# A fused decoder layer on one core: the stacked rows of keys and queries written from SBUF part by part, instead of through a scratch in DRAM

## Chip, core and metric

One core of one Trainium2 chip. The metric is the device time of one launch, in microseconds (us). The profiler's execution is one launch; its span runs from the first to the last instruction.

## What is computed

One decoder layer over 16 items (batches) of 256 tokens and 256 channels: a gated recurrence with quantised weights, cross attention to a context with 16 heads of 16 channels, and a three-layer network; after each a layer norm. The change is in the attention:

```
Q = (query @ Wq.T + bq).reshape(b, sq, H, D).transpose(0, 2, 1, 3)
K = (key @ Wk.T + bk).reshape(b, sk, H, D).transpose(0, 2, 1, 3)
V = (value @ Wv.T + bv).reshape(b, sk, H, D).transpose(0, 2, 1, 3)
Q = apply_rope(Q, cos_q, sin_q)
K = apply_rope(K, cos_k, sin_k)
scores = jnp.einsum('bhqd,bhkd->bhqk', Q, K) * SCALE
scores = jnp.where(mask[:, None, None, :] == 0, neg_inf, scores)
attn = jax.nn.softmax(scores, axis=-1)
out = jnp.einsum('bhqk,bhkd->bhqd', attn, V)
```

## The kernel before

One item g (0 to 15) is one round of a software pipeline; several items are in work at once, and one leaves about every 49.5 us. Every engine runs a fixed list of steps. The list comes from the table `TIMES` (a start time for each step on each engine, relative to `BEGIN[g]`); `order(engine)` sorts the steps of all items by it. The times in the table only set the order; the waits are semaphores. TensorE takes its matmuls strictly in that order.

Keys and queries are float32 after the rotary step and are cut into three bf16 parts whose sum is the value. ScalarE rounds part 0 (step `kp` or `qp`, function `first_part`, L768). VectorE takes the rest and rounds part 1 (`k_parts`, `q_parts`: L1384, L1386, L1400, L1401). Part 2 is the last remainder, for K on GpSimd (`kparts_`, L604), for Q on VectorE (L1402). The tiles `kpart` and `qpart` are [128, 3, 2, 256]: channel c*128+p in partition p of chunk c. A channel index is d*16+h, for d the channel in its head and h the head.

A score is a matmul over stacked rows. `k_st` and `q_st` (two buffers each, for even and odd items) hold in partition 16*s+d, for slot s of six, the part `PARTS_K[s]` or `PARTS_Q[s]` of channel d of all 16 heads: 8 KB for one partition. Row 96 of `k_st` is the mask row. Rows 97 and 98 of `q_st` get the high and low part of the row maximum (`maxrow`, L462, DMAs from `m_hi` and `m_lo`).

`PARTS_Q = (0, 0, 1, 0, 2, 1)` and `PARTS_K = (0, 1, 0, 2, 0, 1)`: part 0 fills three slots, part 1 two, part 2 one.

The stacks are filled by SyncE. `kput` and `qput` (L424, L425) wait for part 2 and write all three parts into a DRAM scratch `scr`, 768 rows of 512 B in one DMA. `kget` and `qget` wait for the landing of that DMA and then issue six DMAs, one for each slot (`stack`, L436): 16 partitions x 8 KB, each partition a contiguous 8 KB in DRAM. `kget` also issues the mask row (L446). The first score tile of an item (`score`, un = 0; its matmuls are L1021) waits for both stacks, `kst_in` and `qst_in`. Later the shifted scores (`shifted`, L1040) wait for `max_in`, the two rows of `maxrow`.

SyncE's order around one item: `loadc`, `maxrow(g-1)`, `kput(g)`, `kget(g)`, `store`, `loadx`, `qput(g)`, `qget(g)`, `loadc`, `maxrow(g)`. A tile of parts is not written again before the scratch DMA that reads it has landed (`kout`, `qout`).

Of the kernel before, what the change touches and what calls it, by code (L numbers as in the profile page):

```python
# [8 lines left out]
BF16 = mybir.dt.bfloat16  # L9
# [3 lines left out]
ALU = mybir.AluOpType  # L13
# [4 lines left out]
P = 128  # L18
NB, S, D = 16, 256, 256
H, DH = 16, 16  # L20
# [4 lines left out]
T = S  # L25
G = NB
NT = T // P
CT = D // P
# [7 lines left out]
PARTS_Q = (0, 0, 1, 0, 2, 1)  # L36
PARTS_K = (0, 1, 0, 2, 0, 1)
# [31 lines left out]
    max2 V62.116 | stat2 G77.947 | round2 V62.352 | rqT P70.375 A74.82 | gate0 P73.784 A75.992 V74.417  # L69
    gate1 P75.073 A76.687 V79.484 | stat3 G95.369 | round3 V80.455 | sqT P81.141 A83.767 | down P83.188 V84.911  # L70
    bn V89.51 G98.004 | x1 V94.309 | kT P64.537 A74.926 | v P55.644 A57.034 | rotk G88.907
    kp A81.655 V82.304 G95.379 | kput S81.174 | kget S97.725 | x1T P84.601 A88.953 | xb G103.696 | q P89.268 A92.187
    rotq G127.27 V96.241 | qp A93.161 V97.684 | qput S116.099 | qget S116.444 | score0 P115.878 V110.409
    score1 P116.97 V115.546 | score2 P119.918 V115.793 | score3 P120.171 V117.492 | score4 P125.547 V117.94
    score5 P126.961 V121.024 | score6 P129.726 V124.461 | score7 P130.83 V124.53 | max P131.852 A132.889 V126.824
    maxrow S133.847 | exp0.0 P133.871 A136.815 | exp0.1 P134.243 A139.205 | pv0 P136.736 | exp1.0 P135.426 A139.693
    exp1.1 P136.729 A139.73 | pv1 P137.231 A141.48 | exp2.0 P137.075 A140.898 | exp2.1 P137.429 A141.482
    pv2 P143.82 | exp3.0 P140.189 A142.702 | exp3.1 P142.471 A144.878 | pv3 P144.83 A145.892
    oTok P146.421 V149.661 | oT P150.162 A147.86 | wo P153.238 V157.354 | bn2 V159.204 G182.428 | x2 V160.758
# [108 lines left out]
def build(nc, A, out):  # L188
    with ExitStack() as ctx:
        def sb(name, shape, dt):  # L190
            return ctx.enter_context(nc.sbuf_tensor(name, shape, dt))

        def sem(name):
            return ctx.enter_context(nc.semaphore(name))

        def count(name, per=1):
            return Count(sem(name), per)
# [64 lines left out]
        kt1 = sb("kt1", [P, 2, T], F32)  # L262
        kt2 = sb("kt2", [P, 2, T], F32)
        krest = sb("krest", [P, CT, T], F32)
        kpart = sb("kpart", [P, 3, CT, T], BF16)
        v_aug = pair("v_aug", [P, NT, H, VW], F32)
        x1T = sb("x1T", [P, CT, T], F32)
        qb = sb("qb", [P, 2, T], F32)
        qt1 = sb("qt1", [P, 2, T], F32)
        qt2 = sb("qt2", [P, 2, T], F32)  # L270
        qrest = sb("qrest", [P, CT, T], F32)
        qpart = sb("qpart", [P, 3, CT, T], BF16)
        q_all = sb("q_st", [P, 2, H, T], BF16)
        k_all = sb("k_st", [P, 2, H, T], BF16)
        q_st = [q_all[:, i] for i in range(2)]
        k_st = [k_all[:, i] for i in range(2)]
# [39 lines left out]
        mneg = oS[0:NB, 1, 0:S // 2].bitcast(BF16)  # L316
        bvT = oS[:, 2:4, 0:P]

        scr = nc.dram_tensor("scr", [2, 2, 3, D, T], BF16).ap()
        mscr = nc.dram_tensor("mscr", [NB * S], BF16).ap()  # L320

# [26 lines left out]
        mx3, sc3, q3 = count("mx3"), count("sc3"), count("q3")  # L349
        mv_s, rstd_s, x1_s, xb_s = (count(n) for n in ("mv_s", "rstd_s", "x1_s", "xb_s"))  # L350
        kt_s, kh_s, kr_s, kp1_s, kparts = (count(n) for n in ("kt_s", "kh_s", "kr_s", "kp1_s", "kparts"))
        qs_s, qr_s, qh_s, qparts = (count(n) for n in ("qs_s", "qr_s", "qh_s", "qparts"))
        kout, qout = count("kout", 16), count("qout", 16)
        kst_in, qst_in = count("kst_in", (len(PARTS_K) + 1) * 16), count("qst_in", len(PARTS_Q) * 16)
        mhi_s, max_in, pv_s = count("mhi_s"), count("max_in", 2 * 16), count("pv_s", 2)
        mv2_s, rstd2_s, x2_s, xh_s = (count(n) for n in ("mv2_s", "rstd2_s", "x2_s", "xh_s"))
        h0h_s, h1h_s = count("h0h_s", KT // 2), count("h1h_s", KT // 2)
# [18 lines left out]
        def _(sp):  # L376
# [40 lines left out]
                sp.wait_ge(mask_s_, 1)  # L417
                sp.dma_start(mscr.rearrange("(b s) -> b s", s=S), mneg).then_inc(mask_out, 16)

            def put(g, n, parts, made, gone):  # L420

                if g >= 2:
                    sp.wait_ge(*(kst_in, qst_in)[n].at(g - 2))
                sp.wait_ge(*made.at(g))  # L424
                sp.dma_start(scr[g % 2, n].rearrange("i (c p) t -> p (i c) t", p=P),  # L425
                             parts[:, :, :, :].rearrange("p i c t -> p (i c) t")).then_inc(gone.sem, 16)

            def kput(g):
                put(g, 0, kpart, kparts, kout)

            def qput(g):
                put(g, 1, qpart, qparts, qout)

            def stack(g, dst, n, which, arrived):
                for s, i in enumerate(which):
                    sp.dma_start(dst[DH * s:DH * (s + 1), :, :],  # L436
                                 scr[g % 2, n, i].rearrange("(d h) t -> d h t", d=DH)).then_inc(arrived.sem, 16)

            def kget(g):
                if g >= 2:  # L440
                    sp.wait_ge(*ringB.filled(g - 2, "exp3.1"))
                if g == 0:
                    sp.wait_ge(mask_out, 16)
                    sp.wait_ge(st_k, 1)
                sp.wait_ge(*kout.at(g))
                sp.dma_start(k_st[g % 2][R_MASK:R_MASK + 1, :, :],  # L446
                             mscr[g * T:(g + 1) * T].rearrange("(o t) -> o t", o=1)
                             .unsqueeze(1).broadcast_to([1, H, T])).then_inc(kst_in.sem, 16)
                stack(g, k_st[g % 2], 0, PARTS_K, kst_in)

            def qget(g):
                if g >= 2:
                    sp.wait_ge(*ringB.filled(g - 2, "exp3.1"))
                if g == 0:
                    sp.wait_ge(st_q, 1)
                sp.wait_ge(*qout.at(g))
                stack(g, q_st[g % 2], 1, PARTS_Q, qst_in)

            def maxrow(g):
                sp.wait_ge(*ringB.emptied(g, "max"))  # L460
# [8 lines left out]
            def later(load):  # L469
                return lambda g: load(g + 2) if g + 2 < G else None  # L470

            steps = {"w:mask": mask_row, "loadx": later(loadx), "loadc": later(loadc), "kput": kput, "kget": kget,
                     "qput": qput, "qget": qget, "maxrow": maxrow, "store": store}
            for step, g in order("SP"):
                steps[step](g)
            sp.wait_ge(*out_s.at(G - 1))
# [2 lines left out]
        def _(pool):  # L479
            own = Own(pool, own_p)  # L480
# [118 lines left out]

            def kparts_(g):  # L600
                if g >= 1:
                    pool.wait_ge(*kout.at(g - 1))
                pool.wait_ge(*kp1_s.at(g))
                pool.tensor_tensor(kpart[:, 2], krest[:, :, :], kpart[:, 1], ALU.subtract).then_inc(kparts.sem, 1)  # L604

# [12 lines left out]
            def norm3(g):  # L618
# [3 lines left out]
                for n in range(NT):  # L622
# [4 lines left out]
            steps = {"w:rope": spread, "w:down": down_weights, "w:wk": lambda g: in_order(w_k, kt1, wkv_in, 2, wk_s), "w:wq": lambda g: in_order(w_q, qt1, wq_in, 1, wq_s),  # L627
                     "scale": scale, "stat1": stat1, "stat2": stat2,
                     "stat3": stat3, "bn": norm1, "xb": xb, "rotk": rotk, "kp": kparts_, "rotq": rotq,
                     "bn2": norm2, "bn3": norm3}  # L630
# [4 lines left out]
        def _(act):  # L635
            own = Own(act, own_a)
# [127 lines left out]
            def first_part(g, turned, t, part, gone, done):  # L764
                if g >= 1:
                    act.wait_ge(*gone.at(g - 1))
                act.wait_ge(*turned.at(g))
                act.activation(part[:, 0], t[:, :, :], ACT.Copy).then_inc(done.sem, 1)  # L768
# [53 lines left out]
            def finish(g):  # L822
                i = g % 2
                act.wait_ge(*rstd3_s.at(g))
                for n in range(NT):
# [4 lines left out]
            steps = {"w:m": lambda g: magnitudes((0, 1), abs_act), "w:g1": sums, "w:g2": lambda g: magnitudes((3, 4), abs_act),  # L830
                     "w:bv": value_bias, "scale": squares1, "xqT": lambda g: unround(g, "xqT", xqT),
                     "iv0": lambda g: input_gate(g, 0), "iv1": lambda g: input_gate(g, 1), "a": decay_raw, "aT": decay,
                     "sq": complement, "rec": squares2, "rqT": lambda g: unround(g, "rqT", rqT),
                     "gate0": lambda g: gate(g, 0), "gate1": lambda g: gate(g, 1),
                     "sqT": sqT_,
                     "w:rope": angles, "w:bqk": qk_bias, "kT": keys, "v": values, "q": queries,
                     "kp": lambda g: first_part(g, kt_s, kt1, kpart, kout, kh_s), "x1T": x1T_,
                     "qp": lambda g: first_part(g, qr_s, qt1, qpart, qout, qh_s), "max": max_high,
                     "pv1": lambda g: weighted(g, 0), "pv3": lambda g: weighted(g, 2), "oT": oT_, "x2T": x2_high,
                     "out": finish}  # L840
            for c in range(KT // 2):
# [337 lines left out]
        def _(dve):  # L1179
            own = Own(dve, own_d)  # L1180
# [199 lines left out]
            def k_parts(g):  # L1380
                if g >= 1:
                    dve.wait_ge(*kparts.at(g - 1))
                dve.wait_ge(*kh_s.at(g))
                dve.tensor_tensor(krest[:, :, :], kt1[:, :, :], kpart[:, 0], ALU.subtract).then_inc(kr_s.sem, 1)  # L1384
                dve.wait_ge(*kr_s.at(g))
                dve.tensor_scalar(kpart[:, 1], krest[:, :, :], 1.0, None, ALU.mult).then_inc(kp1_s.sem, 1)  # L1386
# [8 lines left out]

            def q_parts(g):
                if g >= 1:
                    dve.wait_ge(*qout.at(g - 1))
                dve.wait_ge(*qh_s.at(g))
                own.settle(dve.tensor_tensor(qrest[:, :, :], qt1[:, :, :], qpart[:, 0], ALU.subtract))  # L1400
                own.settle(dve.tensor_scalar(qpart[:, 1], qrest[:, :, :], 1.0, None, ALU.mult))  # L1401
                dve.tensor_tensor(qpart[:, 2], qrest[:, :, :], qpart[:, 1], ALU.subtract).then_inc(qparts.sem, 1)  # L1402

            def score_largest(g, un):
# [120 lines left out]
```

## Time and profile before

| | us |
|---|---|
| median of 3 runs | 890.74 (890.59 to 890.93) |
| the profiled execution, its own time | 888.45 |
| its span | 886.7 |
| TensorE busy | 800.9 |
| VectorE busy | 642.4 |
| ScalarE busy | 549.2 |
| GpSimd busy | 296.9 |

The granted clock of TensorE is 0.998 of full speed over the span. DMA engines are busy for about 30% of it. A busy time is a sum over the whole span; what a wait costs is read in the order of time of one item. Item 8 (its first score at 471 us) stands for the middle of the run.

### The profile page before, as it was taken

Reading aid. Unit: us, or ns where it says so; the run is one execution under the profiler, and the core shown is the slowest. Engines: PE = TensorE matmul, PEld = TensorE weight load, DVE = VectorE, ACT = ScalarE, POOL = GpSimd, SP = SyncE. Lnnn points to the kernel's source line nnn. Section 1 sums busy time; section 2 is a strip of 40 time slices with the busy share of each in tenths; the row PEclk is TensorE's granted clock in tenths of the full one; section 3 lists DMA queues with packets and bytes.
Section 4 is the critical chain, followed back from the end, with each engine's and each line's share of the span. In section 5 each row is a group of like instructions: output and inputs, shape, how many; then the busy total and the mean of one; then the engine's idle time right before and its main releaser. Section 6 shows DMA issues by size and latency. Waiting matters only on the chain.

```text
span 886.7 us, 17907 instructions
## 1 busy us (share of the span) xinstructions
PE 800.9 (90%) x6856; PEld 626.3 (71%) x6890; DVE 642.4 (72%) x1224; ACT 549.2 (62%) x917; POOL 296.9 (33%) x476
## 2 busy tenths in 40 slices
PE   1687899999999999999999999999999999998986
PEld 1444477877877787877878777877777787876665
DVE  6658486886959596886959595977869595966442
ACT  4644857657494847667584848567584948573432
POOL 7753314152333324151433324151423334141001
PEclk9999999999999999999999999999999999999999
DMA  9033332415042332316042433415061423223000
GB/s 298 13 66 66 67 67 51 71 31 115 14 105 41 79 66 56 78 32 114 14 109 36 80 66 56 84 42 98 14 125 21 89 44 63 59 50 72 1 13 25
DMA packets 52517, 57.47 MB, mean 65 GB/s; under 512 B 7856, under 2 KB 48848, under 8 KB 49360
## 3 DMA queue, kind: packets, MB, share of 16 engines
q1 hardware_dynamic: 52432, 56.31, 30.0%
q8 instruction: 56, 0.92, 0.4%
q14 instruction: 29, 0.24, 0.1%
HBM read 39.24 MB, written 16.79 MB: 63 GB/s over the span
## 4 chain that ended last, share of the span: by engine, by line
PE 61%; DVE 16%; ACT 9%; DMA 4%; issue 4%; POOL 3%; SPq 1%; DVEq 0%; ACTq 0%; POOLq 0%
PE bankC L1118 18%; PE bankA L1053 6%; PE bankC L1102 6%; PE bankA L987 6%; PE slotB L1021 6%; PE slotB L1040 5%; PE bankA L922 5%; DMA q_st<-m_lo 4%; DVE u L1304 2%; ACT pr L794 2%; PE bankA L903 2%; DVE bn L1359 2%; ACT sqT L682 2%; ACT L794 2%; POOL rstd L574 2%
## 5 line engine op out<-in xcount | busy, mean ns | idle before, releaser
L1118 PE MATMUL bankC<-h0h,w 128*128 128x256 f16 x1024 | 233.7, 273 | 0.6 <-DVE h0l L1452 0.5
L1118 PE MATMUL bankC<-h0l,w 128*128 128x256 f16 x1024 | 233.3, 272 | 0.0
L1408 DVE TENSOR_REDUCE nmax<-slotB 128x4 f32<-128x1024 f32 x128 | 150.7, 1216 | 1.8 <-PE slotB L1021 0.3
L794 ACT ACTIVATE pr<-slotB 128x1024 f32<-128x1024 f32 x128 | 127.5, 1028 | 13.3 <-PE slotB L1040 13.0
L1118 PEld LDWEIGHTS bankC<-h0h,w 128*128 128x128 f16 x1024 | 99.9, 98 | 15.2 <-issue 1.2
L1118 PEld LDWEIGHTS bankC<-h0l,w 128*128 128x128 f16 x1024 | 100.1, 98 | 14.2
L1040 PE MATMUL slotB<-q_st,k_st 99*128 99x256 bf16 x512 | 74.7, 274 | 13.4 <-DMA q_st<-m_lo 11.2
L573 POOL TENSOR_SCALAR rstd<-mv 128x2 f32<-128x2 f32 x48 | 9.3, 193 | 215.6 <-DVE mv L1362 214.5
L1021 PE MATMUL slotB<-k_st,q_st 97*128 97x256 bf16 x512 | 76.7, 272 | 4.2 <-DVE nmax L1408 2.5
L1040 PEld LDWEIGHTS slotB<-q_st,k_st 99*128 99x128 bf16 x512 | 43.9, 97 | 38.3 <-DMA q_st<-m_lo 15.9
L1102 PE MATMUL bankC<-xh,w 128*128 128x256 f16 x256 | 57.8, 273 | 14.3 <-DVE xl L1446 13.7
L1392 DVE TENSOR_TENSOR qt<-qb,turn 128x512 f32<-128x512 f32 x16 | 11.1, 692 | 76.6 <-ACT qb L751 76.6
L819 ACT ACTIVATE h0h<-bankC 128x512 f16<-128x512 f32 x64 | 38.2, 597 | 44.8 <-PE bankC L1102 44.7
L1053 PE MATMUL bankA<-pr,v_aug 128*32 128x256 f32 x1024 | 65.4, 384 | 0.2 <-ACT pr L794 0.2
L1021 PEld LDWEIGHTS slotB<-k_st,q_st 97*128 97x128 bf16 x512 | 47.8, 97 | 17.9 <-DVE nmax L1408 3.9
L1134 PE MATMUL bankC<-w,h1h 128*128 128x256 f16 x256 | 59.0, 273 | 0.6 <-DVE h1l L1452 0.6
L1134 PE MATMUL bankC<-w,h1l 128*128 128x256 f16 x256 | 59.0, 273 | 0.0
L1102 PE MATMUL bankC<-xl,w 128*128 128x256 f16 x256 | 57.6, 272 | 0.0
L682 ACT ACTIVATE rqT<-bankA,cst 128x512 bf16<-128x512 f16 x16 | 11.0, 687 | 72.4 <-PE bankA L913 72.4
L819 ACT ACTIVATE h1h<-bankC 128x512 f16<-128x512 f32 x64 | 38.0, 594 | 28.9 <-PE bankC L1118 28.9
L1452 DVE SCALAR_TENSOR_TENSOR h1l<-bankC,h1h 128x512 f16<-128x512 f32 x64 | 42.7, 685 | 16.3 <-ACT h1h L819 16.3
L1452 DVE SCALAR_TENSOR_TENSOR h0l<-bankC,h0h 128x512 f16<-128x512 f32 x64 | 43.5, 685 | 6.5 <-ACT h0h L819 4.8
(206 smaller groups left out, 1752.0 us busy)
## 6 DMA issues: line engine op xcount, KB each, us to landing
k_st<-scr SPq DMA_DIRECT2D x96, 128.0 KB, 4.5
q_st<-scr SPq DMA_DIRECT2D x96, 128.0 KB, 4.3
scr<-kpart SPq DMA_DIRECT2D x16, 384.0 KB, 2.8
scr<-qpart SPq DMA_DIRECT2D x16, 384.0 KB, 2.7
x<-in_x SPq DMA_DIRECT2D x16, 256.0 KB, 3.7
cT<-in_ctxT SPq DMA_DIRECT2D x16, 256.0 KB, 2.7
out<-x SPq DMA_DIRECT2D x16, 256.0 KB, 2.2
pr<-in_k SPq DMA_DIRECT2D x1, 1024.0 KB, 9.6
```

The costliest lines, as they stand in the source:

```text
L794: act.activation(pr[i % 2][:, c, :, :].rearrange("p h s -> p (h s)"), slotB[ringB.slot(g, name)][:, :], ACT.Exp, scale=DH ** -0.5).then_in ...
L819: act.activation(flat(dst[:, 2 * m:2 * m + 2, :]), bankC[ringC.slot(g, item)][:, :], ACT.Relu)\
L922: ins = pe.matmul(bankA[ringA.slot(g, name)][:, i * width:(i + 1) * width], xT[:, c, n * P:(n + 1) * P], w[:, c, cols[0]:cols[1]], start=c ...
L987: ins = pe.matmul(bankA[ringA.slot(g, name)][:, e * T:(e + 1) * T], w[:, c, e * P:(e + 1) * P], xT[:, c, :], start=c == 0, stop=c == CT - 1)
L1021: ins = pe.matmul(slotB[ringB.slot(g, f"score{un}")][:, j * T:(j + 1) * T], q_st[g % 2][0:K_SCORE, h, n * P:(n + 1) * P], k_st[g % 2][0:K_ ...
L1040: ins = pe.matmul(slotB[ringB.slot(g, name)][:, j * T:(j + 1) * T], k_st[g % 2][0:K_SHIFTED, h, c * P:(c + 1) * P], q_st[g % 2][0:K_SHIFTE ...
L1053: ins = pe.matmul(bank[j * VW:(j + 1) * VW, half_:half_ + T], v_aug[g % 2][:, c, i * HG + j, :], pr[i % 2][:, c, j, :], start=c == 0, stop ...
L1102: ins = pe.matmul(bankC[ringC.slot(g, name)][:, e * T:(e + 1) * T], w_0[:, c, (2 * m + e) * P:(2 * m + e + 1) * P], a[:, c, :], start=i == ...
L1118: ins = pe.matmul(bankC[ringC.slot(g, name)][:, e * T:(e + 1) * T], w_1[:, i // 2, (2 * m + e) * P:(2 * m + e + 1) * P], (h0h, h0l)[i % 2] ...
L1134: ins = pe.matmul(bankC[ringC.slot(g, "l2.0")][:, n * D:(n + 1) * D], (h1h, h1l)[i % 2][:, i // 2, n * P:(n + 1) * P], w_2[:, i // 2, :], ...
L1408: dve.tensor_reduce(nmax[:, hg * HG * NT + n:(hg + 1) * HG * NT:NT], slotB[ringB.slot(g, name)][:, :].rearrange("p (h s) -> p h s", s=S), ...
L1452: dve.scalar_tensor_tensor(flat(lo[:, two, :]), bankC[ringC.slot(g, item)][:, :], 0.0, flat(hi[:, two, :]), ALU.max, ALU.subtract).then_in ...
```

## The change

The scratch and the steps `kput` and `qput` go. `kget` and `qget` now copy from `kpart` and `qpart` straight into the stacks, SBUF to SBUF. Each slot takes two DMAs, one for each chunk c: 128 rows of 512 B into 8 partitions of 8 KB. So there are twelve DMAs for each stack in place of one and six. They go part by part: the three slots of part 0 when ScalarE has made it (`kh_s`, `qh_s`), the two of part 1 after VectorE (`kp1_s`, and a new `qp1_s`), the one of part 2 after `kparts` or `qparts`. In the table `kget` moves to 85.725 (it was 97.725, with `kput` at 81.174) and `qget` to 113.599 (116.444, with `qput` at 116.099). SyncE's order becomes `loadc`, `maxrow(g-1)`, `kget(g)`, `store`, `loadx`, `qget(g)`, `loadc`. The orders of the other engines are the same as before. The waits before a part tile is written again are for `kst_in` and `qst_in` of the item before; VectorE's `k_parts` gets one more such wait.

```diff
-    kp A81.655 V82.304 G95.379 | kput S81.174 | kget S97.725 | x1T P84.601 A88.953 | xb G103.696 | q P89.268 A92.187
-    rotq G127.27 V96.241 | qp A93.161 V97.684 | qput S116.099 | qget S116.444 | score0 P115.878 V110.409
+    kp A81.655 V82.304 G95.379 | kget S85.725 | x1T P84.601 A88.953 | xb G103.696 | q P89.268 A92.187
+    rotq G127.27 V96.241 | qp A93.161 V97.684 | qget S113.599 | score0 P115.878 V110.409 | score1 P116.97 V115.546
...
-            def put(g, n, parts, made, gone):
-
-                if g >= 2:
-                    sp.wait_ge(*(kst_in, qst_in)[n].at(g - 2))
+            def stack(g, dst, parts, i, which, made, arrived):
+
                 sp.wait_ge(*made.at(g))
-                sp.dma_start(scr[g % 2, n].rearrange("i (c p) t -> p (i c) t", p=P),
-                             parts[:, :, :, :].rearrange("p i c t -> p (i c) t")).then_inc(gone.sem, 16)
...
-            def stack(g, dst, n, which, arrived):
-                for s, i in enumerate(which):
-                    sp.dma_start(dst[DH * s:DH * (s + 1), :, :],
-                                 scr[g % 2, n, i].rearrange("(d h) t -> d h t", d=DH)).then_inc(arrived.sem, 16)
+                for s, part in enumerate(which):
+                    if part == i:
+                        for c in range(CT):
+                            r = DH * s + DH // CT * c
+                            sp.dma_start(dst[r:r + DH // CT, :, :], parts[:, i, c, :]).then_inc(arrived.sem, 16)
...
-                sp.wait_ge(*kout.at(g))
                 sp.dma_start(k_st[g % 2][R_MASK:R_MASK + 1, :, :],
                              mscr[g * T:(g + 1) * T].rearrange("(o t) -> o t", o=1)
                              .unsqueeze(1).broadcast_to([1, H, T])).then_inc(kst_in.sem, 16)
-                stack(g, k_st[g % 2], 0, PARTS_K, kst_in)
+                stack(g, k_st[g % 2], kpart, 0, PARTS_K, kh_s, kst_in)
+                stack(g, k_st[g % 2], kpart, 1, PARTS_K, kp1_s, kst_in)
+                stack(g, k_st[g % 2], kpart, 2, PARTS_K, kparts, kst_in)
...
-                sp.wait_ge(*qout.at(g))
-                stack(g, q_st[g % 2], 1, PARTS_Q, qst_in)
+                stack(g, q_st[g % 2], qpart, 0, PARTS_Q, qh_s, qst_in)
+                stack(g, q_st[g % 2], qpart, 1, PARTS_Q, qp1_s, qst_in)
+                stack(g, q_st[g % 2], qpart, 2, PARTS_Q, qparts, qst_in)
...
             def k_parts(g):
                 if g >= 1:
                     dve.wait_ge(*kparts.at(g - 1))
+                    dve.wait_ge(*kst_in.at(g - 1))
...
             def q_parts(g):
                 if g >= 1:
-                    dve.wait_ge(*qout.at(g - 1))
+                    dve.wait_ge(*qst_in.at(g - 1))
                 dve.wait_ge(*qh_s.at(g))
                 own.settle(dve.tensor_tensor(qrest[:, :, :], qt1[:, :, :], qpart[:, 0], ALU.subtract))
-                own.settle(dve.tensor_scalar(qpart[:, 1], qrest[:, :, :], 1.0, None, ALU.mult))
+                dve.tensor_scalar(qpart[:, 1], qrest[:, :, :], 1.0, None, ALU.mult).then_inc(qp1_s.sem, 1)
+                dve.wait_ge(*qp1_s.at(g))
```

`kparts_` and the two `first_part` steps wait for `kst_in` and `qst_in` of item g-1 in place of `kout` and `qout`.

## Rows read from the trace of the kernel before

**Rows 1.** The page: busy times with their shares, and the chain by engine

```profile
PE 800.9 (90%) x6856; PEld 626.3 (71%) x6890; DVE 642.4 (72%) x1224; ACT 549.2 (62%) x917; POOL 296.9 (33%) x476
PE 61%; DVE 16%; ACT 9%; DMA 4%; issue 4%; POOL 3%; SPq 1%; DVEq 0%; ACTq 0%; POOLq 0%
```

**Rows 2.** Waits, all engines: who waited for whom, us in total, times, longest

```profile
PEld slotB L1040 <- DMA q_st<-m_lo: 15.9, 16, 2.0
```

**Rows 3.** Timeline of SyncE's issues, item 8: start, us, line, out<-in, count

```profile
437.59 0.59 SPq L462 DMA_DIRECT2D q_st<-m_lo  x1
444.13 0.38 SPq L425 DMA_DIRECT2D scr<-kpart  x1
...
447.47 2.88 SPq L436 DMA_DIRECT2D k_st<-scr  x6
...
454.74 0.96 SPq L387 DMA_DIRECT2D x<-in_x  x1
459.82 0.36 SPq L425 DMA_DIRECT2D scr<-qpart  x1
462.62 3.66 SPq L436 DMA_DIRECT2D q_st<-scr  x6
```

**Rows 4.** Timeline of TensorE at the first score, items 0, 1, 5, 8, 15

```profile
76.41 1.03 PE L1021 MATMUL slotB<-k_st,q_st 97*128 97x256 bf16 x8
...
123.61 0.60 PE L1021 MATMUL slotB<-k_st,q_st 97*128 97x256 bf16 x4 [0.62 <-issue]
...
321.89 0.60 PE L1021 MATMUL slotB<-k_st,q_st 97*128 97x256 bf16 x4
...
471.08 0.60 PE L1021 MATMUL slotB<-k_st,q_st 97*128 97x256 bf16 x4
...
816.00 0.60 PE L1021 MATMUL slotB<-k_st,q_st 97*128 97x256 bf16 x4 [0.83 <-issue]
```

**Rows 5.** Timelines of ScalarE, VectorE, GpSimd: the steps that make the parts

```profile
63.46 0.63 ACT L768 ACTIVATE qpart<-qt 128x512 bf16<-128x512 f32 x1 [0.30 <-DVE qt L1394]
...
109.75 0.63 ACT L768 ACTIVATE qpart<-qt 128x512 bf16<-128x512 f32 x1 [0.29 <-DVE qt L1394]
...
308.37 0.63 ACT L768 ACTIVATE qpart<-qt 128x512 bf16<-128x512 f32 x1
...
437.67 0.62 ACT L768 ACTIVATE kpart<-kt 128x512 bf16<-128x512 f32 x1
...
456.99 0.63 ACT L768 ACTIVATE qpart<-qt 128x512 bf16<-128x512 f32 x1
...
802.78 0.63 ACT L768 ACTIVATE qpart<-qt 128x512 bf16<-128x512 f32 x1 [0.81 <-DVE qt L1394]
...
459.05 0.69 DVE L1402 TENSOR_TENSOR qpart<-qrest,qpart 128x512 bf16<-128x512 f32 x1
...
442.90 1.16 POOL L604 TENSOR_TENSOR kpart<-krest,kpart 128x512 bf16<-128x512 f32 x1
```

**Rows 6.** Q issues of items 9, 15; us to landing: first, last of each, m_lo

```profile
512.12 2.63 SPq L436 DMA_DIRECT2D q_st<-scr  x6
...
808.45 2.63 SPq L436 DMA_DIRECT2D q_st<-scr  x6
...
q_st<-scr SPq DMA_DIRECT2D x1, 128.0 KB, 3.1
...
q_st<-scr SPq DMA_DIRECT2D x1, 128.0 KB, 5.8
...
q_st<-scr SPq DMA_DIRECT2D x1, 128.0 KB, 5.3
...
q_st<-m_lo SPq DMA_DIRECT2D x1, 8.0 KB, 1.8
```

**Rows 7.** One-microsecond windows: scratch write, then a Q stack; last: DMA share, GB/s

```profile
461.00:462.00 1.00, 1.00 (x8) 0.80 (x7) 0.60 (x2) 0.98 (x3) 0.00 (x0) 1.00 0.96 290
515.00:516.00 1.00, 1.00 (x11) 0.91 (x10) 0.93 (x4) 0.00 (x0) 0.00 (x0) 1.00 1.05 131
```

More of the change, by code:

```diff
@@ L71 @@
     bn V89.51 G98.004 | x1 V94.309 | kT P64.537 A74.926 | v P55.644 A57.034 | rotk G88.907
-    kp A81.655 V82.304 G95.379 | kput S81.174 | kget S97.725 | x1T P84.601 A88.953 | xb G103.696 | q P89.268 A92.187
-    rotq G127.27 V96.241 | qp A93.161 V97.684 | qput S116.099 | qget S116.444 | score0 P115.878 V110.409
-    score1 P116.97 V115.546 | score2 P119.918 V115.793 | score3 P120.171 V117.492 | score4 P125.547 V117.94
-    score5 P126.961 V121.024 | score6 P129.726 V124.461 | score7 P130.83 V124.53 | max P131.852 A132.889 V126.824
-    maxrow S133.847 | exp0.0 P133.871 A136.815 | exp0.1 P134.243 A139.205 | pv0 P136.736 | exp1.0 P135.426 A139.693
+    kp A81.655 V82.304 G95.379 | kget S85.725 | x1T P84.601 A88.953 | xb G103.696 | q P89.268 A92.187
+    rotq G127.27 V96.241 | qp A93.161 V97.684 | qget S113.599 | score0 P115.878 V110.409 | score1 P116.97 V115.546
+    score2 P119.918 V115.793 | score3 P120.171 V117.492 | score4 P125.547 V117.94 | score5 P126.961 V121.024
+    score6 P129.726 V124.461 | score7 P130.83 V124.53 | max P131.852 A132.889 V126.824 | maxrow S133.847
+    exp0.0 P133.871 A136.815 | exp0.1 P134.243 A139.205 | pv0 P136.736 | exp1.0 P135.426 A139.693
     exp1.1 P136.729 A139.73 | pv1 P137.231 A141.48 | exp2.0 P137.075 A140.898 | exp2.1 P137.429 A141.482
@@ L317, in build @@
         bvT = oS[:, 2:4, 0:P]
-        scr = nc.dram_tensor("scr", [2, 2, 3, D, T], BF16).ap()
         mscr = nc.dram_tensor("mscr", [NB * S], BF16).ap()
@@ L351, in build @@
         kt_s, kh_s, kr_s, kp1_s, kparts = (count(n) for n in ("kt_s", "kh_s", "kr_s", "kp1_s", "kparts"))
-        qs_s, qr_s, qh_s, qparts = (count(n) for n in ("qs_s", "qr_s", "qh_s", "qparts"))
-        kout, qout = count("kout", 16), count("qout", 16)
-        kst_in, qst_in = count("kst_in", (len(PARTS_K) + 1) * 16), count("qst_in", len(PARTS_Q) * 16)
+        qs_s, qr_s, qh_s, qp1_s, qparts = (count(n) for n in ("qs_s", "qr_s", "qh_s", "qp1_s", "qparts"))
+        kst_in, qst_in = count("kst_in", (len(PARTS_K) * CT + 1) * 16), count("qst_in", len(PARTS_Q) * CT * 16)
         mhi_s, max_in, pv_s = count("mhi_s"), count("max_in", 2 * 16), count("pv_s", 2)
@@ L418, in mask_row @@
                 sp.dma_start(mscr.rearrange("(b s) -> b s", s=S), mneg).then_inc(mask_out, 16)
-            def put(g, n, parts, made, gone):
-                if g >= 2:
-                    sp.wait_ge(*(kst_in, qst_in)[n].at(g - 2))
+            def stack(g, dst, parts, i, which, made, arrived):
                 sp.wait_ge(*made.at(g))
-                sp.dma_start(scr[g % 2, n].rearrange("i (c p) t -> p (i c) t", p=P),
-                             parts[:, :, :, :].rearrange("p i c t -> p (i c) t")).then_inc(gone.sem, 16)
[L428 to L432, printed above, removed]
-            def stack(g, dst, n, which, arrived):
-                for s, i in enumerate(which):
-                    sp.dma_start(dst[DH * s:DH * (s + 1), :, :],
-                                 scr[g % 2, n, i].rearrange("(d h) t -> d h t", d=DH)).then_inc(arrived.sem, 16)
+                for s, part in enumerate(which):
[3 more added lines that the diff above has]
+                            sp.dma_start(dst[r:r + DH // CT, :, :], parts[:, i, c, :]).then_inc(arrived.sem, 16)
             def kget(g):
@@ L470, in later @@
                 return lambda g: load(g + 2) if g + 2 < G else None
-            steps = {"w:mask": mask_row, "loadx": later(loadx), "loadc": later(loadc), "kput": kput, "kget": kget,
-                     "qput": qput, "qget": qget, "maxrow": maxrow, "store": store}
+            steps = {"w:mask": mask_row, "loadx": later(loadx), "loadc": later(loadc), "kget": kget,
+                     "qget": qget, "maxrow": maxrow, "store": store}
             for step, g in order("SP"):
@@ L601, in kparts_ @@
                 if g >= 1:
-                    pool.wait_ge(*kout.at(g - 1))
+                    pool.wait_ge(*kst_in.at(g - 1))
                 pool.wait_ge(*kp1_s.at(g))
@@ L836, in _ @@
                      "w:rope": angles, "w:bqk": qk_bias, "kT": keys, "v": values, "q": queries,
-                     "kp": lambda g: first_part(g, kt_s, kt1, kpart, kout, kh_s), "x1T": x1T_,
-                     "qp": lambda g: first_part(g, qr_s, qt1, qpart, qout, qh_s), "max": max_high,
+                     "kp": lambda g: first_part(g, kt_s, kt1, kpart, kst_in, kh_s), "x1T": x1T_,
+                     "qp": lambda g: first_part(g, qr_s, qt1, qpart, qst_in, qh_s), "max": max_high,
                      "pv1": lambda g: weighted(g, 0), "pv3": lambda g: weighted(g, 2), "oT": oT_, "x2T": x2_high,
```

## The prediction, made before the changed kernel was run

> **What bounds the kernel now.** I read the page first, then the chain of work that ended last, then the order of time around the first score tile of an item. An item is one of the 16 batches; g counts them from 0. The page shows TensorE busy for 90% of the span, and the chain is 61% TensorE [rows 1]. So the kernel is a stream of matmuls in a fixed order, and anything outside TensorE counts only where that stream stops for it. Two places concern the stacks. First, the weight load of the first shifted score waits in all 16 items for `q_st<-m_lo` [rows 2]; that is `maxrow`, which the change leaves alone but sets a new neighbour. Second, the first score tile (L1021) waits for `k_st` and `q_st`. K has slack: its stack is issued from 447.47 [rows 3] and wanted at 471.08 [rows 4]. Q has none. The last of six Q DMAs of item 15 is issued 0.42 us before the end of its group, at 810.66, and takes 5.3 us, so it lands at 815.96; the score starts at 816.00 after 0.83 us idle, put down to "issue" [rows 4, 6]. In item 1 the idle is 0.62. In item 9 the same sum gives 514.33 + 5.8 = 520.1, and the score of that item starts less than half a microsecond later. The Q stack therefore lands just in time now: the one number that decides this change is when the new Q stack lands.
>
> **Step 1, the scratch goes.** Now Q is written to DRAM as one DMA when its last part is ready, issued at 459.82, and the stack is issued at 462.62, 2.80 us later [rows 3]. After the change the first halves go as soon as part 0 is ready: ScalarE ends it at 456.99 + 0.63 = 457.62 [rows 5]. That is 5.00 us before the present first issue. Part 1 is ready by 459.05, where VectorE begins part 2, which is ready at 459.05 + 0.69 = 459.74 [rows 5]. Six halves (part 0 fills three slots) need 6 x 0.44 = 2.6 us of issue (six take 2.63 to 3.66 now [rows 3, 6]), until 460.3, so neither later part is waited for. All twelve are issued by about 457.7 + 12 x 0.44 = 463.0, if an issue costs what it does now.
>
> **Step 2, the transfers.** Six DMAs of 16 partitions x 8 KB become twelve of 8 partitions x 8 KB, read from 128 rows of 512 B. Call T the spacing between two landings of these halves. No row shows such a transfer, so I bound it. From below: a write of the scratch reads the same 512 B rows, and all 16 engines together move 290 GB/s at a share of 0.96 [rows 7], that is 302 / 16 = 18.9 GB/s for one. A half is shared among eight engines at most if each takes whole partitions of the target, so 65.5 KB / (8 x 18.9) = 0.43 us; the issue rate of 0.44 gives the same. From above: if reading those rows (0.43) and writing them did not overlap, 0.43 + 0.93 = 1.36. Between: a stack DMA of 128 KB takes, by its landings, from 808.45 + 3.1 to 815.96 for five more, 0.88 us each in item 15, and from 512.12 + 3.1 to 520.13, 0.98 each in item 9 [rows 6]. I take T = 0.91, near the lower of these, because the halves alternate between two groups of eight partitions and can only overlap a little, and the DRAM read is gone.
>
> A small DMA from SBUF to SBUF lands 1.8 us after issue [rows 6]. So from "part 0 ready" to the last landing: 0.05 + 1.8 + 12 T = 1.85 + 12 T, which is 12.77 us at T = 0.91.
>
> The Trainium skill speaks against this change at this place. Its page "SBUF — State Buffer", section "Door 1: The DMA port swizzle", gives 27.2 GB/s for each port and four partitions per port in a row, so 16 neighbouring partitions reach four ports and 8 reach two. By it a half takes 65.5 / 54.4 = 1.20 us (an estimate from the page). It would also make the present DMA take 1.20 us, and the rows show 0.88 to 0.98, so the measured rate is a quarter to a third above the page's; the grouping may still hold. "DMA: Bandwidth & Descriptors", section "Why a DMA increments its semaphore by 16 and not by 1", would put each half on eight engines; no run here shows it.
>
> **Step 3, the budget.** From the end of part 0 on ScalarE to the start of the first score: item 8, 471.08 - 457.62 = 13.46 us, and ten items are within 0.2 of it; item 5, 321.89 - 309.00 = 12.89, as in items 2 and 12. Without their present idle, item 1 has 123.61 - 110.38 - 0.62 = 12.61 and item 15 has 816.00 - 803.41 - 0.83 = 11.76. Item 0, where filler matmuls stand ahead of the score, has 76.41 - 64.09 = 12.32 [rows 4, 5]. Against 12.77: thirteen items pay nothing; item 15 is 1.01 late instead of 0.83 (+0.18), item 1 0.16 instead of 0.62 (-0.46), item 0 0.45 late. Sum +0.2 us.
>
> **Step 4, what else moves.** K: part 0 ends on ScalarE at 438.29, part 2 on GpSimd at 442.90 + 1.16 = 444.06 [rows 5]. The last K half lands by 438.7 + 1.8 + 12 x 0.91 = 451.4, twenty microseconds early, and before `loadx` at 454.74. SyncE stands in `kget` from 438.2 to about 445 instead of waiting in `kput`; the steps behind it, `store` and `loadx`, were not due before 454 [rows 3], so nobody waits. In `qget` it stands from 455.7 to 463, where now it ends at 466.3, so `loadc` behind it is not held. The waits of ScalarE, VectorE and GpSimd for the stack of the item before (instead of the scratch write) look at something that landed over 30 us earlier, and cost nothing while it does. VectorE's extra wait in `k_parts` and the changed one in `q_parts` are one semaphore instruction each. The DRAM traffic saved was on no path.
>
> **Against the times.** The profiled execution took 888.45 us (span 886.7); the median is 890.74, 2.29 more. 888.45 + 0.2 + 2.29 = 890.9.
>
> **Rivals.**
> *Late on arrival (slower).* The halves come slower than T = 0.967 and the ten items, too, find TensorE waiting; each further 0.1 us of T costs 1.2 us in every item. The sum over the items: T = 0.94, +2.0 us; 0.98, +6.5; 1.05, +20; 1.10, +30. For it: the target's rate is 0.88 to 0.98 now, 512 B rows cost the engines more than 8 KB runs, and every engine serves the queue in order. Against: reads leave DRAM. Times 892.7 to 920. Chance 0.26. Its far end, T = 1.20 (the rate of a target of 8 partitions a quarter below what item 15's landings give), lands 16.25 us after part 0 and costs about 49 us: 939.7; rows so far speak against such a rate. Chance 0.08. It is what the 27.2 GB/s a port of the Trainium skill's page "SBUF — State Buffer" would give.
> *Halves side by side (faster).* If the two groups of eight partitions take writes at the same time, or DRAM was the limit, T = 0.44: 7.1 us, six early. TensorE's order is fixed, so only the idle of items 1 and 15 goes, -1.45: 889.3. That is 0.16%; a little more if other executions wait oftener than the profiled one. Chance 0.16, half of it above 0.2%.
> *A neighbour for m_lo (slower).* The K stack's mask row and first halves are now issued right behind `m_lo` (437.59 [rows 3]), where nothing was issued until 444.13. If they hold its landing up by d, all 16 items pay d, since TensorE waits for it each time; from d = 0.11 it is measurable, at 0.3 it gives 895.5. Against: the first half is issued at 438.7, and m_lo lands at 439.4. Chance 0.06.
>
> **How the numbers follow.** Forecast (T from 0.88 to 0.935, 890.0 to 892.4) 0.44; the others 0.26, 0.08, 0.16, 0.06. About 0.2% is what a measurement of this kernel can tell from no change, 1.8 us. Faster by more: 0.08. Within: 0.44 + 0.08 = 0.52. Slower: 0.26 + 0.08 + 0.06 = 0.40. The range runs from 889.0 (below the side-by-side case's 889.3) to 912 (T a little over 1.05, which gives 910.7); it leaves out the far end, 0.08, the upper part of the late case, some 0.07, and 0.04 below.
>
> **What would show it.** In the trace after: twelve Q issues of 64 KB from about 457.7 in item 8's time, 0.44 apart; the last landing near 470.5; L1021 idle before it (now 0.62 and 0.83 in two items, else none) near zero. The wait for m_lo at 1.0 us an item as now. I am wrong if L1021 is preceded by idle in most items (T above 0.967), if an issue of a half costs over 0.9 us (then the issues set T), if m_lo takes over 1.9 us in the middle of the run, or if the period of 49.5 us changes with none of these.

## The result and the profile after

The changed kernel takes 912.29 us in the median of 4 runs (910.42 to 918.97); the kernel before, run beside it, 890.66. The ratio is 1.0256, with a 95% interval of 1.0202 to 1.031: 2.6% slower. The profiled execution took 910.97 us against 888.45 before, 22.5 more; its span grew by 22.3, from 886.7 to 909.0.

The page of the changed kernel, the lines that answer to [rows 1] and the two groups that changed most (line, operation, count | busy, mean ns | idle before it and what ended most of it):

```profile
span 909.0 us, 18025 instructions
PE 807.0 (89%) x6856; PEld 630.9 (69%) x6890; DVE 645.7 (71%) x1224; ACT 549.2 (60%) x917; POOL 296.8 (33%) x476
...
HBM read 14.08 MB, written 4.20 MB: 20 GB/s over the span
...
L1011 PE MATMUL slotB<-k_st,q_st 97*128 97x256 bf16 x512 | 76.9, 273 | 20.5 <-issue 17.0
L1030 PE MATMUL slotB<-q_st,k_st 99*128 99x256 bf16 x512 | 75.9, 277 | 15.0 <-DMA q_st<-m_lo 12.7
```

L1011 is the score matmul that was L1021, L1030 the shifted one. The scratch traffic is gone as the diff says, and nothing became faster by it. TensorE's idle time before the first score is now 17.0 us in 12 items, put down to "issue", and 2.8 in one more; before it was 0.62 + 0.83 in two items [rows 4]. That is 18.3 us more. TensorE is also 6.1 us longer busy with the same 6856 matmuls. Together this is 24.4 us, a little over the 22.3 of the span. The lists of TensorE's waits show the rest: `m_lo` now costs 12.7 us instead of 11.2, while the waits for `nmax` at the first score fell from 2.5 to 0.8 and one for `bcol` at the start of the launch from 3.0 to 1.5. Not all of the 6.1 us belongs to the change, as the part on the clock below shows.

Timeline of the changed kernel, SyncE's Q issues of item 8 and its neighbours, the end of part 0 on ScalarE, and TensorE at the first score of items 8, 12, 13 and 15; they answer to [rows 3 to 5]:

```profile
470.40 7.85 SPq L425 DMA_DIRECT2D q_st<-qpart  x12
...
520.69 8.20 SPq L425 DMA_DIRECT2D q_st<-qpart  x12
...
469.70 0.63 ACT L758 ACTIVATE qpart<-qt 128x512 bf16<-128x512 f32 x1
...
484.73 0.60 PE L1011 MATMUL slotB<-k_st,q_st 97*128 97x256 bf16 x4 [0.78 <-issue]
...
686.09 0.60 PE L1011 MATMUL slotB<-k_st,q_st 97*128 97x256 bf16 x4 [2.25 <-issue]
...
735.87 0.60 PE L1011 MATMUL slotB<-k_st,q_st 97*128 97x256 bf16 x4
...
837.15 0.60 PE L1011 MATMUL slotB<-k_st,q_st 97*128 97x256 bf16 x4 [3.12 <-issue]
```

Part 0 of item 8 is ready at 470.33, the first half is issued at 470.40, and twelve issues take 7.85 us: 0.65 each, not 0.44. The first score comes at 484.73, 14.40 us after part 0. The budget was 13.46, and TensorE stands for 0.78 us. The item now takes about 50.3 us (470.40 to 520.69) in place of 49.5. Item 8 is one of the milder ones: where TensorE waits, the first score follows part 0 by 13.88 us (item 9) to 15.31 (item 12).

Windows of the changed kernel: eight microseconds in the middle of that Q stack, then six after the first score of item 15 (the last three columns are granted clock, DMA share, GB/s):

```profile
474.00:482.00 8.00, 7.10 (x56) 6.00 (x55) 7.23 (x16) 4.37 (x9) 0.89 (x2) 1.00 0.66 67
837.00:843.00 6.00, 5.84 (x37) 4.39 (x38) 3.28 (x4) 1.19 (x2) 0.00 (x0) 0.72 0.01 3
```

The stack moves 67 GB/s, so a half of 65.5 KB takes 0.98 us here; by the landing, (14.40 - 1.85) / 12 = 1.05. This is the T of the prediction. Over all items that wait, the same formula gives T = 1.00 to 1.12.

### The profile page after: what moved, and what is told of

Its sections match the earlier page's. It is cut to its first block, busy times and chain, and to the rows that moved or that the text cites. A ratio compares the mean times of both kernels' runs of the same rounds, so it can differ in the third digit from the quotient of the medians.

```text
span 909.0 us, 18025 instructions
## 1 busy us (share of the span) xinstructions
PE 807.0 (89%) x6856; PEld 630.9 (69%) x6890; DVE 645.7 (71%) x1224; ACT 549.2 (60%) x917; POOL 296.8 (33%) x476
## 4 chain that ended last, share of the span: by engine, by line
PE 62%; DVE 13%; ACT 9%; DMA 5%; issue 5%; POOL 3%; SPq 2%; DVEq 0%; ACTq 0%; POOLq 0%
PE bankC L1108 17%; PE bankC L1092 6%; PE bankA L1043 6%; PE bankA L977 6%; PE slotB L1011 6%; PE slotB L1030 6%; PE bankA L912 5%; DMA q_st<-m_lo 3%; DVE u L1294 2%; ACT pr L784 2%; PE bankA L893 2%; DVE bn L1349 2%; ACT L784 1%; ACT sqT L672 1%; POOL rstd L564 1%
## 5 line engine op out<-in xcount | busy, mean ns | idle before, releaser
L1011 PE MATMUL slotB<-k_st,q_st 97*128 97x256 bf16 x512 | 76.9, 273 | 20.5 <-issue 17.0
L1030 PE MATMUL slotB<-q_st,k_st 99*128 99x256 bf16 x512 | 75.9, 277 | 15.0 <-DMA q_st<-m_lo 12.7
L1011 PEld LDWEIGHTS slotB<-k_st,q_st 97*128 97x128 bf16 x512 | 47.8, 97 | 35.9 <-issue 23.2
L1030 PEld LDWEIGHTS slotB<-q_st,k_st 99*128 99x128 bf16 x512 | 44.0, 98 | 40.9 <-DMA q_st<-m_lo 17.4
L528 POOL TENSOR_SCALAR st<-st 128x2 f32<-128x2 f32 x32 | 6.2, 193 | 131.5 <-ACT junk L709 130.2
```

The lines of the kernel that those rows point to most:

```text
L1011: ins = pe.matmul(slotB[ringB.slot(g, f"score{un}")][:, j * T:(j + 1) * T], q_st[g % 2][0:K_SCORE, h, n * P:(n + 1) * P], k_st[g % 2][0:K_ ...
L1030: ins = pe.matmul(slotB[ringB.slot(g, name)][:, j * T:(j + 1) * T], k_st[g % 2][0:K_SHIFTED, h, c * P:(c + 1) * P], q_st[g % 2][0:K_SHIFTE ...
```

## The experiments

There were two questions: whether the Q stack alone is late, and what makes a half take 1.0 us. My theory after the result was that a group of about eight neighbouring target partitions takes only some 65 to 75 GB/s. The rivals were the 512 B rows read out of SBUF, the issue cost of 0.65, and a disturbance by the K stack.

**Q alone, K alone.** From the changed kernel, one of the two stacks was given back its scratch, with the waits and table entries that belong to it. Core of the edit for `q_direct`:

```diff
-                stack(g, k_st[g % 2], kpart, 0, PARTS_K, kh_s, kst_in)
-                stack(g, k_st[g % 2], kpart, 1, PARTS_K, kp1_s, kst_in)
-                stack(g, k_st[g % 2], kpart, 2, PARTS_K, kparts, kst_in)
+                from_scratch(g, k_st[g % 2], 0, PARTS_K, kst_in)
```

> Only Q goes straight from its parts to the stack (twelve halves); K keeps the scratch, its put and its six DMAs. Theory (the Q stack lands late, K is off the path): all of the loss stays, 908 to 914 us, with idle before L1011-like first score tiles in most items, and a first score about 14.4 us after part 0 of Q. Rival (the K halves behind m_lo, or K's longer hold of the queue, cost the time): near the kernel before, 889 to 892.

> Only K goes straight; Q keeps the scratch and six DMAs. Theory (Q alone is late): as before, 890 to 892 us, the wait for m_lo still 1.0 us an item, and the first score not later than before. Rival (K's halves delay m_lo or others): 900 or more.

`q_direct` took 914.68 us, ratio 1.0274 (1.0223 to 1.0326): the whole loss, with idle before the first score in 14 of the 16 items. `k_direct` took 891.84, ratio 1.0012 (0.9996 to 1.0028): no measurable difference. The waits of both (who waited for whom, us in total, times, longest), first `q_direct`:

```profile
PE slotB L1027 <- issue: 18.6, 13, 2.9
PE slotB L1046 <- DMA q_st<-m_lo: 13.3, 16, 1.7
PE slotB L1027 <- DMA q_st<-qpart: 3.3, 1, 3.3
```

and `k_direct`:

```profile
PEld slotB L1027 <- issue: 4.5, 7, 1.4
PE slotB L1046 <- DMA q_st<-m_lo: 12.3, 16, 1.4
```

L1027 is the first score's line in both. With Q direct the idle before it is 21.9 us; with K direct the weight load waits 4.5 us in 7 items, against 2.7 in 4 in the kernel before. The wait for `m_lo` in `k_direct`, where the K halves stand right behind it, is 12.3 us, in the kernel before 11.2 by the same view: at most 0.07 us an item. K is off the path, and its new place costs nearly nothing.

**Spreading the targets.** In the changed kernel, two lines say where a half goes:

```diff
-                            r = DH * s + DH // CT * c
-                            sp.dma_start(dst[r:r + DH // CT, :, :], parts[:, i, c, :]).then_inc(arrived.sem, 16)
+                            r = CT * s + c
+                            sp.dma_start(dst[r:R_MASK:12, :, :], parts[:, i, c, :]).then_inc(arrived.sem, 16)
```

> As the changed kernel, but the rows of both stacks are ordered so that one half's 8 target partitions lie 12 apart instead of side by side (row = 12*i + 2*s + c, for channel pair i, slot s and chunk c); both stacks use the same order, so every score is the same sum. Theory A (a group of neighbouring target partitions limits the write, T = 1.0 us a half): now only the issue rate of 0.66 us limits, the DMA windows show about 100 GB/s instead of 65, Q lands about 1.9 + 12 x 0.66 = 9.8 us after part 0, no idle at the first score, 888.5 to 890 us. Theory B (eight engines, or the 512 B rows read in SBUF, limit): the windows stay at 65 GB/s and the time at 909 to 914.

888.70 us, ratio 0.9974 (0.9958 to 0.999), against 1.0256 for the same kernel with neighbouring targets. Windows of `spread` in a Q stack; the last two columns are DMA share and GB/s:

```profile
511.00:517.00 6.00, 6.00 (x47) 5.25 (x46) 5.02 (x12) 3.53 (x8) 0.89 (x2) 1.00 0.36 98
```

98 GB/s at a share of 0.36, where the changed kernel had 67 at 0.66. The same bytes, the same 128 source rows of 512 B, the same number of target partitions; only their distance differs. 98 GB/s is 65.5 KB in 0.67 us, the rate of the issues. So theory B is out: the source rows, and the engines that one half can use, allow at least this rate. A limit on each single partition is out too, since there are still eight.

**How near is too near.** In `step2` the eight partitions lie 2 apart, within the 16 rows of the slot:

```diff
+                            sp.dma_start(dst[DH * s + c:DH * (s + 1):CT, :, :], parts[:, i, c, :]).then_inc(arrived.sem, 16)
```

> The changed kernel with the 8 target partitions of a half 2 apart, within the 16 rows of its slot (row = 16*s + 2*i + c). If the limit belongs to groups of about four neighbours (16 neighbours reach four groups, 8 reach two), four groups are reached and T falls to the issue rate of 0.66: idle at the first score gone, 888 to 892. If it belongs to a larger group of 16 or more, nothing is gained: 65 GB/s and 908 to 915.

889.54 us, ratio 0.9986 (0.9969 to 1.0004); no wait at the first score is put down to "issue" or to a DMA. A window in its Q stack:

```profile
510.00:516.00 6.00, 6.00 (x42) 5.21 (x41) 4.93 (x13) 4.46 (x10) 0.90 (x2) 1.00 0.34 93
```

Reaching across 16 rows instead of 8 is enough. The limit belongs to groups smaller than 16 neighbours. Whether such a group is four rows or eight, this does not tell: here a half touches two aligned groups of eight, so either size fits.

**Sixteen partitions a half.** `wide` sends a half to 16 neighbouring partitions, 4 KB each. It computes other scores, so it is a probe and no kernel to keep:

```diff
+                            h = H // CT * c
+                            sp.dma_start(dst[DH * s:DH * (s + 1), h:h + H // CT, :],
+                                         parts[:, i, c, :]).then_inc(arrived.sem, 16)
```

> As the changed kernel, but each half goes to 16 neighbouring partitions of 8 heads (4 KB each) instead of 8 partitions of 16 heads. That puts channels in other heads' rows, so it computes other scores; bytes, rows of 512 B and number of DMAs are the same. Theory A (the target group limits: 16 partitions take 128 KB in 0.9): T near the issue rate, no idle at the first score, 888.5 to 891. It also tells the issue cost: if 0.66 us comes from the target's first dimension of 8, an issue takes about 0.44 here. Theory B (reading 512 B rows from SBUF limits whatever the target): 65 GB/s again, 909 to 914.

889.76 us, ratio 0.9986 (0.9967 to 1.0006), at 99 GB/s:

```profile
515.00:521.00 6.00, 6.00 (x43) 5.20 (x42) 4.91 (x14) 4.26 (x10) 0.89 (x2) 1.00 0.39 99
...
512.37 7.87 SPq L425 DMA_DIRECT2D q_st<-qpart  x12
```

Theory A holds again. The side guess on the issue was wrong: with a target dimension of 16, twelve issues still take 7.87 us, 0.66 each.

**Halves in the kernel before.** The other way round: the old kernel, scratch and all, with each stack DMA split in two.

```diff
-                    sp.dma_start(dst[DH * s:DH * (s + 1), :, :],
-                                 scr[g % 2, n, i].rearrange("(d h) t -> d h t", d=DH)).then_inc(arrived.sem, 16)
+                    for c in range(CT):
+                        r = DH * s + DH // CT * c
+                        sp.dma_start(dst[r:r + DH // CT, :, :],
+                                     scr[g % 2, n, i, c * P:(c + 1) * P].rearrange("(d h) t -> d h t", d=DH // CT))\
+                          .then_inc(arrived.sem, 16)
```

> The kernel before, with scratch and puts, but each of the six stack DMAs split into two halves of 8 partitions, still contiguous 8 KB runs in DRAM: twelve halves for K and for Q. Theory (a group of 8 neighbouring target partitions takes about 65 GB/s whatever the source): 1.0 us a half, Q lands about 1.9 + 12 x 1.0 = 13.9 us after the first issue, that is near 476.5 in item 8's time instead of 471.0, late by 5.4 us in most items: 960 to 975 us. Rival (the 512 B rows out of SBUF are what is slow): a half of 8 KB runs takes half of 0.93, the time stays at 889 to 893. It also tells whether an issue on a target of 8 partitions costs 0.66 us with a DRAM source (now 0.44 with 16 partitions).

Two runs took 959.16 and 978.59 us, just below and just above the range that I gave; with two runs this far apart there is no interval. The kernel before takes 890.5 on this chip. The profile is of the run of 959.16 us, 69 over it. Here are the page's busy line, then item 9: Q's issues, the first score, and windows over the stack and behind the first score.

```profile
PE 822.4 (86%) x6856; PEld 640.0 (67%) x6890; DVE 649.4 (68%) x1224; ACT 549.3 (57%) x917; POOL 296.4 (31%) x476
...
501.00 4.45 SPq L438 DMA_DIRECT2D q_st<-scr  x12
...
512.60 0.60 PE L1024 MATMUL slotB<-k_st,q_st 97*128 97x256 bf16 x4 [3.28 <-issue]
...
504.00:511.00 7.00, 4.41 (x38) 3.41 (x35) 5.91 (x9) 3.09 (x8) 0.64 (x2) 1.00 0.49 76
513.00:515.00 2.00, 2.00 (x15) 1.53 (x14) 1.77 (x3) 0.60 (x1) 0.00 (x0) 0.67 0.00 0
515.00:517.00 2.00, 2.00 (x10) 1.56 (x9) 1.97 (x6) 0.60 (x1) 0.02 (x1) 0.50 0.00 0
```

With contiguous 8 KB runs out of DRAM, eight neighbouring partitions still take only 76 GB/s, where whole DMAs on 16 neighbours had 131 [rows 7]. So the target limits with either source. The source of 512 B rows in SBUF makes it some 12% worse (67); whether the short rows do that or the place, no run tells apart. In item 9 the first score comes 11.60 us after the first issue, so T = (11.60 - 1.85) / 12 = 0.81, below the 1.0 that I expected; over the 16 items it is 0.63 to 0.90. Q is late by 3.28 us in item 9, not by 5.4. The rest of the time is the clock: after this idle time TensorE's granted clock is 0.67 over two microseconds, then 0.50, which is 1.2 of 2.4 GHz, and TensorE is 822.4 us busy instead of 800.9. The idle before the first score is 47.6 + 6.2 us by the waits; less 1.45, plus 21.5 of longer work, that is 73.8, against 70.7 us of longer span. So Q was less late than forecast, and the time came out near the range by what the clock added, which the forecast had not counted. An issue costs 0.34 to 0.37 here, so a target of eight partitions does not by itself make it 0.66. What does was not separated: the scratch write also reads 128 rows of SBUF and takes 0.36, but writes DRAM, and the small `m_lo` copy from SBUF to SBUF takes 0.59 [rows 3].

**Spreading the kernel before.** One edit in the old kernel, in both stacks: `dst[s:R_MASK:len(PARTS_K), :, :]` in place of `dst[DH * s:DH * (s + 1), :, :]`.

> The kernel before with one change: the 16 target partitions of a stack DMA lie 6 apart (row = 6*d + s) in both stacks. Theory (the target group limits the old stack DMAs too): the DMA windows go from 131 to over 200 GB/s, six DMAs land at the issue rate of 0.44, Q about 2 us earlier, the idle of items 1 and 15 (0.62 and 0.83) goes: 1.5 us under the kernel before, 0.2%. Rival (DRAM limits the old stack DMAs): 131 GB/s and no change.

889.29 us, ratio 0.9982 (0.9969 to 0.9996). The DMA issues of `before_spread`, KB each and median us from issue to landing:

```profile
q_st<-scr SPq DMA_DIRECT2D x96, 128.0 KB, 2.6
```

The page of the kernel before has 4.3 there. Part of that comes from issues further apart (six take 3.66 us in item 9, before 2.63), so the whole stack is the fairer measure: in item 9 it lands 5.67 us after its first issue (518.58 + 2.6 - 515.51), in the kernel before 8.01. That is about the 2 us that were forecast. The old stack DMAs, too, were held by their 16 neighbouring targets, and Q's lateness in items 1 and 15 was the price: no wait at the first score is put down to "issue" or to a DMA any more. Expected were 200 GB/s; in item 9 the windows show 115 to 148 in most microseconds and 262 in one, as they do in the kernel before, so this forecast failed and the windows do not show the gain.

> The spread version again, beside before_spread on one chip: 0.997 to 0.998 of the kernel before. Theory: it and before_spread are equal within 0.1%, since both have Q in time and the rest is TensorE's order.

889.41 us, ratio 0.9991 (0.9975 to 1.0007), on the same chip as `before_spread`: equal to it within 0.1%. Over both chips `spread` is 0.1 to 0.3% under the kernel before. Its gain is real on the first chip and inside the uncertainty on the second.

**Ten halves.** The changed kernel with one Q slot left out, so that the term of part 1 against part 1 is missing from the scores. The core of the edit:

```diff
-                stack(g, q_st[g % 2], qpart, 1, PARTS_Q, qp1_s, qst_in)
+                stack(g, q_st[g % 2], qpart, 1, PARTS_Q[:5], qp1_s, qst_in)
```

A constant, written once at the start, stands in the unwritten rows.

> The changed kernel with ten Q halves instead of twelve: the last Q slot (part 1 against K's part 1) is not written and keeps a constant, so that small term of every score is another one; everything else is the same. Theory (Q lands 1.85 + n T after its part 0, T = 1.0 to 1.05): n = 10 gives 11.9 to 12.4 us against a budget of 12.9 to 13.5, so the idle at the first score goes in all items but the first and the last, 889 to 893 us. Rival (the loss comes with direct copies as such, whatever their number): 905 or more.

890.97 us, ratio 1.0014 (0.9998 to 1.003). Two halves fewer, with the targets still neighbouring, and the loss is gone. The waits of `ten_halves_b`:

```profile
PEld slotB L1011 <- issue: 3.4, 4, 1.8
```

Four items still wait, item 15 by 1.8 us and item 0 by 1.0, as the shorter budgets of the first and last items say.

## Why the prediction was wrong

**The place was right.** Everything was made to hang on the landing of Q against the start of the first score, with K, `m_lo` and the DRAM traffic off the path. `q_direct` and `k_direct` show just that. The rival of the neighbour for `m_lo` is not borne out: 0.07 us an item in `k_direct` and 0.09 in the changed kernel (12.7 against 11.2 us in all).

**The term that was mis-sized is T, in step 2.** I took 0.91 us a half. It is 0.98 by the window and 1.05 by the landing in item 8, and 1.00 to 1.12 over the items that wait. The reasons that I gave for taking the lower side were that the halves alternate between two groups of partitions and that the DRAM read is gone. The runs show what these are worth. With 8 KB runs out of DRAM, eight neighbours take a half in 0.81 in item 9 (`before_halves`), so the alternation seems to bring something against 0.93; no run kept all halves on one group, so this is argued. But the 512 B rows in SBUF cost more than that: 67 GB/s instead of 76. So leaving DRAM was a loss and not a gain. I had this against me in the text ("512 B rows cost the engines more than 8 KB runs") and gave it no number. Break-even was T = 0.967. A change that turns on 6% of an unmeasured rate has no business with a forecast of "no change" as its likeliest case.

**The budget held, and the sum with some luck.** Budgets of 13.46, 12.89 and so on gave +20 us at T = 1.05; the idle before the first score grew by 18.3. Item 12, with the shorter budget, waits 2.25, and item 15 3.12, the longest. Nine of the 13 items that wait had a T above 1.05, and items 6, 11 and 13, which do not wait at all, make up for it. In each of these three, one of the later issues took 1.48 to 1.90 us in place of 0.61 to 0.65, and the windows behind it rise from 62 to 64 up to 92 to 105 GB/s. Item 13, where the issue at 729.40 took 1.90:

```profile
726.00:727.00 1.00, 1.00 (x9) 0.80 (x8) 0.81 (x2) 0.98 (x3) 0.00 (x0) 1.00 0.66 64
732.00:733.00 1.00, 0.63 (x6) 0.32 (x4) 0.97 (x3) 0.94 (x2) 0.00 (x0) 1.00 0.62 105
```

Item 12, the slowest, stays at 57 to 62 GB/s from 674 us to its end. Item 8 of `q_direct`, whose 12 issues take 8.97 us, does not wait either. So T is not fixed by the shape of a half alone. Perhaps a pause lets writes to two groups of rows overlap. No run tested this, and it stays open.

**The clock is a smaller part, and most of it is not the change's.** I counted idle time only. In the changed kernel the granted clock falls at the two ends of the run: 0.67 over three microseconds after item 0's wait of 2.8 us, 0.50 to 0.52 from 98 to 104 us, where the pipeline is still filling, and 0.72 over six microseconds after item 15's first score. TensorE's work is 6.1 us longer. But `wide` and `before_spread`, where Q is never late, show falls at the same early places, from 82 us and near 100, and TensorE is busy 805.1 and 805.5 us in them, at medians of 889.76 and 889.29. The profiled execution of the kernel before has no such fall (800.9 us, mean clock 0.998), while most of its other launches have a mean clock of 0.994 to 0.996. So the early falls come with and without the late Q, and the 2.29 us between the profiled execution and the median already holds some of them. Of the changed kernel's falls, only the one behind item 15 has no counterpart in a kernel that has Q in time. Nor does the length of an idle time tell whether the clock falls after it. Two places of `q_direct`, each with the first score and the three microseconds behind it, and then `wide`:

```profile
636.68 0.49 PE L1027 MATMUL slotB<-k_st,q_st 97*128 97x256 bf16 x3 [2.10 <-issue]
637.00:640.00 3.00, 3.00 (x18) 2.22 (x16) 2.69 (x4) 0.60 (x1) 0.00 (x0) 0.56 0.00 0
...
690.19 0.60 PE L1027 MATMUL slotB<-k_st,q_st 97*128 97x256 bf16 x4 [2.89 <-issue]
690.00:693.00 3.00, 2.81 (x26) 2.60 (x27) 2.09 (x3) 1.44 (x5) 0.73 (x2) 1.00 0.03 5
...
82.00:85.00 3.00, 3.00 (x16) 1.65 (x14) 1.96 (x2) 1.42 (x3) 1.61 (x2) 0.55 0.00 0
```

The spread of the runs goes with the clock: the four of the changed kernel have mean clocks of 0.986 to 0.992, the slowest the lowest. At T = 1.05 the sum gives 910.7, the range ended at 912, and the median is 912.29. The idle time alone, 18.3 us, would have stayed inside the range; how much of the last microseconds is the change's clock and how much that of the launches was not separated.

**Step 1 was right in its times and wrong in the issue.** The first half goes 0.07 us after part 0. An issue costs 0.65 us, not 0.44. It did not matter at T of 1.0; in `spread` it is the limit.

**The Trainium skill's rules.** "SBUF — State Buffer", section "Door 1: The DMA port swizzle", puts four neighbouring partitions on one port and moves to the next port with the next four. `step2`, `spread` and `wide` agree with it: 8 neighbours reach two ports, 16 rows four. They would agree with groups of eight as well. Its figure of 27.2 GB/s a port would give 54 for the halves, an estimate from that page; measured are 67 and 76. These are rates of a stream whose halves alternate between two groups of rows, so they do not show the figure itself to be too low. I used the gap in the figure to discount the rule, and the grouping was the part that counted.

## What to carry to other kernels

Before a transfer is split or narrowed, look at which target partitions one DMA touches: eight neighbours took 67 to 76 GB/s here, eight rows spread by 2 or by 12 took 93 to 98, and there the issues set the pace. Where the row order of a contraction is free, try a strided target: here it cost nothing (888.70 and 889.54 us) and the limit was gone. And where something lands within 1 us of its use, give the unmeasured rate a number from both sides and let the break-even decide the forecast.

## What was not expected of the hardware

A DMA from 128 rows of 512 B in SBUF into SBUF takes SyncE 0.65 us to issue, whether it writes 8 or 16 partitions; one from DRAM into 8 partitions takes 0.34 to 0.37, one from SBUF into DRAM with 768 rows 0.36 [rows 3]. Which property of the copy sets this stays open. The distance of eight target rows alone changed the rate from 67 GB/s side by side to 93 and 98 with steps of 2 and 12.

TensorE's clock does not follow the length of an idle time alone: it stayed at its full level after 2.25 us in the changed kernel, 2.63 in `before_halves` and 2.89 in `q_direct`, and fell to 0.56 after 2.10 in `q_direct`. In `before_halves` 52 us of added waiting came with 21.5 us of longer work, 71 us of time in all.
